# Scores and state products on four quarters of the array, and the second tile's state products next to the last chunk's scores

## The chip, the cores and the metric

The kernel runs on one core of a Trainium2 chip. The metric is the device time of one launch in microseconds (us), the median of several runs.

## The reference

One layer of a network on x of 4 sequences x 2048 tokens x 512 features: an attention with decaying state (32 heads of 16 features, chunks of 64 tokens), then a feed-forward part of 2048 hidden units. Cut to what matters, for one chunk and all heads:

```
att = rc @ kc * w_mat                  # scores, 64 x 64 per head, masked by decay
yc  = att @ vc + rc @ state * wb       # from the chunk, and from the state before it
new_state = ws * state + kc * wk @ vc  # the state product of the chunk ("kv")
```

r, k, v and a gate g come from four projections of mixed, normalized tokens; y is normalized per head, gated, projected by Wo and added to x; the feed-forward part is `x + gelu(norm(x) @ W0.T + b0) @ W1.T + b1`. The state is zero at the start of each sequence.

## The kernel before

The work goes in 32 steps of 256 tokens (`BT`), each of two tiles t of 128 tokens, each of two chunks of 64 tokens, so four chunks c = 0 to 3 a step. The attention of step n stands in one loop body with the feed-forward part of step n - 2 and with the tail (gate, Wo, residual) of step n - 1: `in_step` (L739) says what a step has, and 35 steps are issued in all. The order of each engine's work is written out by hand: `pe_step` (L1134) for TensorE, `dve_steady` (L1401) and `dve_step` for VectorE, `act_steady` (L1742) for ScalarE, `pool_step` for GpSimd, `sp_steady` (L2024) for the DMA queue of SyncE. Engines meet at counting semaphores (`s_...`). Products in higher precision than 16 bits are made as three passes over high and low halves (`PASSES`).

Features are spread over the 128 partitions so that k and r of a group g (8 heads; four groups) have the even heads of the group on partitions 0 to 63 and the odd heads on 64 to 127, for every group alike. `sp_stack` (L1981) copies them by DMA into `kx` and `rx`, with zeros between heads.

The small matmuls, which the change touches, and how they use the array of 128 rows (contracted partitions) by 128 columns (output partitions):

- Scores, `pe_scores` (L912, matmul in L926), once a chunk: 32 matmuls of 64 rows, 64 columns and 64 moving elements. The even head of a pair goes from rows 0 to 63 into columns 0 to 63, the odd one from rows 64 to 127 into columns 64 to 127. The first 16 fill one PSUM bank of `sc` (x = 0), the next 16 the other (x = 1), each half with its own wait on the weighing of the chunk before (`s_am`) and its own signal (`s_sc`).
- Attention times values, `pe_att_v` (L931, L947 and L950), once a tile: 64 matmuls of 128 rows and 64 columns, with 64 and 32 moving elements in turn. They write banks 0 and 2 of the PSUM tensor `YT`. Bank 2 (`T32`) also takes the state product of a tile's first chunk, so the group waits for that chunk's masking on VectorE (`s_km`, count 2t + 1).
- From the state, `pe_from_state` (L955, L966), right behind: 24 matmuls of 128 rows, 64 columns and 128 moving elements into bank 1, where the state product of the second chunk had been (wait on `s_km`, 2t + 2).
- State products, `pe_kv` (L971, L990), once a tile: 24 matmuls of 64 rows (a chunk's tokens), 128 columns and 128 moving elements. They give, for each group of 8 heads, all products of 128 by 128 features, also those between different heads.

In a steady step TensorE's order around them is: up 3, scores 0, kv of tile 0, G, up 4, scores 1, up 5, G, up 6, attention and from-state of tile 0, scores 2, up 7, Wo, kv of tile 1, down 0, scores 3, down 1, Wo, down 2, attention and from-state of tile 1, down 3 ("up" is L1045, 16 matmuls of 128x256; "down" is L1109, 8 of 128x512; G and the other projections are L864 and L896; Wo is L1017).

VectorE takes the scores (`dve_weigh`, L1310) and splits them (`dve_weights_lo`, L1316), and for the state of each chunk (`dve_state`, L1319) multiplies the 128x512 product by `headmask`, which leaves the products within a head (L1327, L1329 for the last chunk), and adds it to the faded state in four instructions of 128x128 (L1341). ScalarE (L1696) and GpSimd (L1942) copy the state `S` of 128x512 into 16-bit halves `Shl`. `dve_take_y` (L1352) weighs the part from the state (L1357) and adds the two from the chunk (L1365, L1367).

Before the steps, `prepare` loads and transposes the weights; `load` (L455) brings the matrices of k and r in four DMAs each, one a group, in the feature order named above.

Of the kernel before, what the change touches and what calls it, by code (L numbers as in the profile page):

```python
# [8 lines left out]
ALU = mybir.AluOpType  # L9
# [72 lines left out]

def by_head(ap):
    return ap.rearrange("p (h d) -> p h d", h=H)

def program(nc, ctx, a, consts, x, out, wd, nb):
# [34 lines left out]
    headmask = sb("headmask", [P, P])  # L122
# [27 lines left out]
    YT = ps("YT", [P, 3, C])  # L150
    Y = YT[:, 0:2, :]
# [272 lines left out]
    def prepare():  # L424
# [8 lines left out]
        tabs = sb("tabs", [P, 3 * Q + 2 + 8], F32, own)  # L433
        dist, after, same = (tabs[:, Q * k:Q * k + Q] for k in range(3))
        ages = tabs[:, 3 * Q:3 * Q + 2]
        mine = tabs[:, 3 * Q + 2:3 * Q + 10]
# [15 lines left out]
        def full(u):  # L452
            return 16 * G if u in (K_, R_) else 16
# [62 lines left out]
        def dve_exponents(eng):  # L516
            eng.wait_ge(s_tab, 48)
            eng.tensor_scalar(wb[:, :], en[:, :], ages[:, 0:1], None, ALU.mult).then_inc(s_n, 1)
            eng.tensor_scalar(wk[:, :], en[:, :], ages[:, 1:2], None, ALU.mult).then_inc(s_n, 1)
            for p in range(2):  # L520
                half = slice(Q * p, Q * p + Q)
                eng.tensor_copy(up[half, :], un[half, p:H:2]).then_inc(s_n, 1)
            eng.tensor_tensor(en_mine[:, :, :], en[:, :].rearrange("p (g h) -> p g h", g=G),
                              mine.unsqueeze(1).to_broadcast([P, G, 8]), ALU.mult).then_inc(s_n, 1)
# [180 lines left out]
    kv = sb("kv", [P, C])  # L705
    S = sb("S", [P, C])
    Shl = sb("Shl", [P, 2, 2, C], F16)
# [51 lines left out]
    def pe_piece_mean(eng, k):  # L759

        eng.wait_ge(s_ones, 1)
        if k == 0:
            eng.wait_ge(s_psq, PIECES)
            eng.wait_ge(s_wlo, 9)
            sums = f_sum[:, 0:PIECES]
        else:
            eng.wait_ge(s_yi, NT)
            eng.wait_ge(s_pm, 1)
            sums = f_most[:, :]
# [117 lines left out]
    def pe_V(eng, n, t):  # L887
        if due(NT * n):
            eng.wait_ge(s_yi if t else s_y, NT * n)
# [22 lines left out]
    def pe_scores(eng, n, c):  # L912
# [5 lines left out]
        for x in range(2):  # L918
            if c:
                eng.wait_ge(s_am, 8 * n + 2 * (c - 1) + x + 1)  # L920
            for gg in range(2):
                g = 2 * x + gg
                for q in range(4):
                    for p in range(2):
                        head = slice(Q * p, Q * p + Q)
# [3 lines left out]
            mm.then_inc(s_sc, 1)  # L929

    def pe_att_v(eng, n, t):  # L931
# [23 lines left out]
    def pe_from_state(eng, n, t):  # L955

        eng.wait_ge(s_km, NCH * n + 2 * t + 2)
# [4 lines left out]
        for g in range(G):  # L962
            for i, (a, b) in enumerate(PASSES):
                for cc in range(2):
                    at = P * t + Q * cc
                    mm = eng.matmul(Y[Q * cc:Q * cc + Q, 1, rows(g)], rT[:, a, g, at:at + Q],  # L966
                                    Shl[:, cc, b, rows(g)], start=(i == 0), stop=(i == 2))
                    if g == G - 1 and i == 2:
                        mm.then_inc(s_in, 1)

    def pe_kv(eng, n, t, ahead):  # L971
# [162 lines left out]
    def pe_step(eng, n):  # L1134
# [184 lines left out]
    def dve_state(eng, n, c):  # L1319
# [4 lines left out]
        src = (Y[:, 1, :] if c % 2 else T32).rearrange("p (g c) -> p g c", g=G)  # L1324
        mask = headmask[:, :].unsqueeze(1).to_broadcast([P, G, P])
# [26 lines left out]
    def dve_take_y(eng, n, t):  # L1352
        eng.wait_ge(s_in, NCH * n + 2 * t + 2)
        eng.wait_ge(s_av, NCH * n + 2 * t + 2)
        if due(NT * n + t):
            eng.wait_ge(s_gs, NT * n + t)
        eng.tensor_tensor(by_head(yi[:, :]), by_head(Y[:, 1, :]), wb[:, :].unsqueeze(2).to_broadcast([P, H, N]),  # L1357
                          ALU.mult).then_inc(s_yi, 1)
# [3 lines left out]
        halves = YT[:, 0:3:2, :].rearrange("p k (q b d) -> p k q b d", q=8, b=2)  # L1362
# [821 lines left out]
def constants():  # L2184
# [4 lines left out]
    spread = 32 * (r % 4) + N * (r // Q) + r % Q // 4  # L2189
# [3 lines left out]
        "headmask": same_head[spread],  # L2193
        "tabs": np.concatenate([
            np.maximum(i - j - 1, 0), (i > j) * ATT_S, (i == j) * ATT_S, -(r % Q)[:, None], -(Q - 1 - r % Q)[:, None],
            2 * (r % 4)[:, None] + r[:, None] // Q == np.arange(8)[None, :]], 1).astype(np.float32),
# [23 lines left out]
```

## Time and profile before

| | |
|---|---|
| median of 3 runs | 2111.5 us (2108.79 to 2116.0) |
| span of the profiled execution (first to last instruction) | 2113.0 us; its time apart from the span is not given |
| TensorE: matmuls / weight loads busy | 98% / 70% |
| VectorE / ScalarE / GpSimd busy | 85% / 62% / 18% |
| DMA queue of SyncE, share of 16 engines | 76.5% |
| TensorE's granted clock, mean | 0.995 |

Busy time of TensorE is a sum over matmuls whose ends are modelled and which overlap; the distance from the start of one group to the start of the next says what room a group takes. A clock of 1 is 2.4 GHz, one of 0.5 is 1.2 GHz. "Idle before" is time in which an engine had nothing running, with what ended it.

### The profile page before, as it was taken

The page shows a single profiled execution, that of the slowest core. Times are in us where ns is not written, and L with a number is a line of the kernel's source. Part 1 is how long each engine was busy: PE and PEld are TensorE (multiplying, and loading weights), DVE is VectorE, ACT ScalarE, POOL GpSimd, SP SyncE. Part 2 cuts the span into 40 slices and gives each one's busy share as a digit, 9 for nine tenths or more (in the row PEclk, how much of TensorE's full clock was granted, in tenths as well). Part 3 has the DMA queues.
Part 4 walks back from the last instruction along what each step waited for, and adds up shares of the span by engine and source line. Part 5 has one row for each costly group of instructions (what it writes and reads, how often), then busy time and mean ns, then how long its engine had stood idle before and what let it go on. Part 6 is the DMA issues. An engine that isn't in the chain of part 4 may idle for free.

```text
span 2113.0 us, 58603 instructions
## 1 busy us (share of the span) xinstructions
PE 2063.0 (98%) x24134; PEld 1479.5 (70%) x24134; DVE 1804.0 (85%) x3623; ACT 1320.0 (62%) x2081; POOL 388.0 (18%) x329
## 2 busy tenths in 40 slices
PE   5989999999999999999999999999999999999998
PEld 5777667777766777766777776676776677777665
DVE  7889889888888989888988988898988889898761
ACT  7876556667655667665656765666766566676442
POOL 1111111221211121111122111112221211211120
PEclk8999999999999999999999999999999999999999
DMA  6977777788776788777778877777887777887676
GB/s 211 229 193 234 185 217 220 224 245 235 210 215 212 225 239 241 224 209 220 218 223 245 236 216 214 223 223 224 245 232 198 227 214 222 243 236 213 206 248 231
DMA packets 428892, 471.61 MB, mean 223 GB/s; under 512 B 259409, under 2 KB 309329, under 8 KB 428625
## 3 DMA queue, kind: packets, MB, share of 16 engines
q1 hardware_dynamic: 426992, 467.64, 76.5%
q8 instruction: 192, 3.15, 0.6%
q14 instruction: 76, 0.61, 0.1%
q10 hardware_dynamic: 1632, 0.21, 0.1%
HBM read 316.24 MB, written 25.17 MB: 162 GB/s over the span
## 4 chain that ended last, share of the span: by engine, by line
PE 89%; DVE 3%; ACT 2%; DMA 2%; SPq 2%; issue 1%; ACTq 0%; DVEq 0%
PE F L1109 20%; PE F L1045 19%; PE B L864 11%; PE B L1017 8%; PE sc L864 7%; PE YT L896 7%; PE YT L864 3%; PE sc L926 3%; PE YT L947 2%; PE YT L990 2%; PE YT L966 2%; PE YT L1045 1%; PE F L821 1%; DMA y<-ygT 1%; PE YT L950 1%
## 5 line engine op out<-in xcount | busy, mean ns | idle before, releaser
L1109 PE MATMUL F<-ring,hT 128*128 128x512 f16 x1984 | 468.0, 380 | 0.0
L1045 PE MATMUL F<-xT,ring 128*128 128x256 f16 x3840 | 450.1, 273 | 6.6 <-issue 3.9
L1045 PEld LDWEIGHTS F<-xT,ring 128*128 128x128 f16 x3840 | 369.9, 98 | 66.3 <-issue 9.5
L1109 PEld LDWEIGHTS F<-ring,hT 128*128 128x128 f16 x1984 | 186.7, 98 | 195.3
L1739 ACT ACTIVATE hT<-F,b,f_rho 128x256 f16<-128x256 f32 x480 | 243.8, 560 | 81.8 <-PE F L1045 81.8
L1942 POOL TENSOR_TENSOR Shl<-S,Shl 128x512 f16<-128x512 f32 x128 | 156.4, 1222 | 739.8 <-ACT Shl L1696 739.8
L864 PE MATMUL B<-mix,WT 128*128 128x256 f16 x2304 | 267.6, 273 | 1.2 <-DVE gT L1348 1.2
L1696 ACT ACTIVATE Shl<-S 128x512 f16<-128x512 f32 x128 | 80.6, 630 | 283.0 <-PE YT L966 161.0
L864 PEld LDWEIGHTS B<-mix,WT 128*128 128x128 f16 x2304 | 222.6, 98 | 36.4 <-DVE gT L1348 1.5
L267 DVE SCALAR_TENSOR_TENSOR mixf<-dx,maa,xnT 128x256 f32<-128x256 f32 x512 | 238.8, 527 | 0.1
L1316 DVE TENSOR_TENSOR att<-att 128x512 f16<-128x512 f32 x256 | 180.2, 745 | 16.0 <-ACT att L1690 15.9
L327 DVE TENSOR_TENSOR mix<-mixf,mix 128x1024 f16<-128x1024 f32 x128 | 184.1, 1438 | 2.7 <-ACT mix L323 1.6
L864 PE MATMUL sc<-mix,WT 128*128 128x256 f16 x1536 | 179.6, 274 | 2.9 <-PEq L551 2.9
L896 PE MATMUL YT<-WT,mix 128*128 128x512 f16 x768 | 177.8, 382 | 1.1 <-DVE mix L327 0.7
L1017 PE MATMUL B<-WT,yg 128*128 128x512 f16 x768 | 176.2, 379 | 0.0
L1310 DVE TENSOR_TENSOR att<-sc,wmask 128x512 f32<-128x512 f32 x256 | 164.3, 684 | 12.8 <-PE sc L926 12.8
L864 PEld LDWEIGHTS sc<-mix,WT 128*128 128x128 f16 x1536 | 150.8, 98 | 34.0 <-issue 3.1
L1947 POOL TENSOR_TENSOR x<-e,x 128x512 f32<-128x512 f16 x62 | 70.8, 1162 | 556.4 <-DVE e L1383 556.4
L1690 ACT ACTIVATE att<-att 128x512 f16<-128x512 f32 x256 | 147.2, 623 | 19.0 <-DVE att L1310 17.7
L1341 DVE SCALAR_TENSOR_TENSOR S<-S,ws,kv 128x128 f32<-128x128 f32 x384 | 142.8, 433 | 3.9 <-POOL Shl L1942 0.5
L323 ACT ACTIVATE mix<-mixf 128x1024 f16<-128x1024 f32 x128 | 134.4, 1050 | 4.8 <-DVE mixf L267 3.9
L896 PEld LDWEIGHTS YT<-WT,mix 128*128 128x128 f16 x768 | 75.2, 98 | 86.3 <-issue 2.6
(196 smaller groups left out, 3066.9 us busy)
## 6 DMA issues: line engine op xcount, KB each, us to landing
ring<-w_dram SPq DMA_DIRECT2D x512, 512.0 KB, 4.6
kx<-kT SPq DMA_DIRECT2D x96, 256.0 KB, 3.9
rx<-rT SPq DMA_DIRECT2D x96, 256.0 KB, 4.5
xa<-in_L_attn_x SPq DMA_DIRECT2D x32, 512.0 KB, 7.2
vbd<-vN SPq DMA_DIRECT2D x256, 64.0 KB, 2.9
x<-in_L_attn_x SPq DMA_DIRECT2D x32, 512.0 KB, 6.2
out<-x SPq DMA_DIRECT2D x31, 512.0 KB, 4.0
w_dram<-ring SPq DMA_DIRECT2D x20, 256.0 KB, 3.8
```

What stands on the lines that cost most here:

```text
L267: last = eng.scalar_tensor_tensor(out=mixf[:, m % 2, g, :], in0=dx[:, g, :], scalar=maa[:, m, g:g + 1], in1=xnT[:, g, 1:BT + 1], op0=ALU.m ...
L327: eng.tensor_tensor(mix[:, m % 2, 1, :, :], mixf[:, m % 2, :, :], mix[:, m % 2, 0, :, :], ALU.subtract).then_inc(s_ml, 1)
L864: mm = eng.matmul(out[:, gg * BT:(gg + 1) * BT], WT[:, w, a, kk, rows(g)], mix[:, m % 2, b, kk, :], start=(i == 0 and kk == 0), stop=(i == ...
L896: mm = eng.matmul(Y[:, t, :], mix[:, 0, a, kk, rows(t)], WT[:, V_, b, kk, :], start=(i == 0 and kk == 0), stop=(i == 2 and kk == G - 1))
L1017: mm = eng.matmul(B[:, :], yg[:, a, kk, rows(t)], WT[:, O_, b, kk, :], start=(i == 0 and kk == 0), stop=(i == 2 and kk == G - 1))
L1045: mm = eng.matmul(up_place(f, j)[:, i * BT:(i + 1) * BT], ring[:, use % RING, i, a * C + kk * P:a * C + (kk + 1) * P], xT[:, :, kk, :], st ...
L1109: mm = eng.matmul(F[:, t, :], hT[:, k, rows(t)], ring[:, use % RING, i, a * C:(a + 1) * C], start=(k == 0 and a == 0), stop=(k == NH - 1 a ...
L1310: eng.tensor_tensor(att32[:, x, :], sc[:, x, :], wmask[:, 8 * x:8 * x + 8, :].rearrange("p q i -> p (q i)"), ALU.mult).then_inc(s_am, 1)
L1316: eng.tensor_tensor(att[:, c % 2, 1, C * x:C * x + C], att32[:, x, :], att[:, c % 2, 0, C * x:C * x + C], ALU.subtract).then_inc(s_al, 1)
L1690: eng.activation(att[:, c % 2, 0, C * x:C * x + C], att32[:, x, :], ACT.Copy).then_inc(s_ah, 1)
L1739: eng.activation(hT[:, k, :], up_place(f, j)[:, i * BT:(i + 1) * BT], ACT.Gelu, bias=b0[:, k:k + 1], scale=f_rho[:, j:j + 1]).then_inc(s_h, 1)
L1942: eng.tensor_tensor(Shl[:, b, 1, :], S[:, :], Shl[:, b, 0, :], ALU.subtract).then_inc(s_Sl, 1)
```

## The change

Scores, from-state and kv matmuls all become 64 rows by 64 columns with 64 moving elements, and follow one another over the four quarters of the array. For groups 2 and 3 the even heads now lie on partitions 64 to 127 and the odd ones on 0 to 63 (`rows_of`). From-state and kv go from 24 matmuls to 48; the state and its product keep only the rows and columns of one parity, so `kv`, `S` and `Shl` are half as wide (256 in place of 512). The PSUM tensor `YT` is divided anew, the attention group waits for both chunks' masking, and `dve_take_y` weighs in two instructions. The kv of tile 1 moves from behind Wo to behind down 0, directly ahead of scores 3. The first two weight matrices are loaded in six DMAs each. Tables (`headmask`, `tabs`) follow the new feature order; their part of the diff is left out.

```diff
+def rows_of(g, p):
+    half = p if g < 2 else 1 - p
+    return slice(Q * half, Q * half + Q)
...
     YT = ps("YT", [P, 3, C])
+    BY_PARITY = YT[:, :, :].rearrange("p b c -> p (b c)").rearrange("p (k s c) -> p k s c", k=2, s=3)
+    FROM_STATE = BY_PARITY[:, :, 0, :]
+    FROM_CHUNK = BY_PARITY[:, :, 1:3, :].rearrange("p k s c -> p k (s c)")
...
         def load(eng, u):
...
                 for b in range(G):
-                    eng.dma_start(raw[:, u, b, :], source[b]).then_inc(landed[u], 16)
+                    if b < 2:
+                        eng.dma_start(raw[:, u, b, :], source[b]).then_inc(landed[u], 16)
+                    else:
+                        for p in range(2):
+                            at = rows_of(b, p)
+                            eng.dma_start(raw[at, u, b, :], source[b][N * p:N * p + N]).then_inc(landed[u], 16)
...
-    kv = sb("kv", [P, C])
-    S = sb("S", [P, C])
-    Shl = sb("Shl", [P, 2, 2, C], F16)
+    kv = sb("kv", [P, C // 2])
+    S = sb("S", [P, C // 2])
+    Shl = sb("Shl", [P, 2, 2, C // 2], F16)
...
     def pe_V(eng, n, t):
         if due(NT * n):
-            eng.wait_ge(s_yi if t else s_y, NT * n)
+            eng.wait_ge(s_y, NT * n)
...
     def pe_scores(eng, n, c):
...
-        for x in range(2):
-            if c:
-                eng.wait_ge(s_am, 8 * n + 2 * (c - 1) + x + 1)
-            for gg in range(2):
-                g = 2 * x + gg
-                for q in range(4):
+        if c:
+            eng.wait_ge(s_am, 8 * n + 2 * c)
+        for gg in range(2):
+            for q in range(4):
+                for x in range(2):
                     for p in range(2):
-                        head = slice(Q * p, Q * p + Q)
+                        g = 2 * x + gg
+                        head = rows_of(g, p)
                         mm = eng.matmul(sc[Q * p:Q * p + Q, x, gg * BT + Q * q:gg * BT + Q * q + Q],
                                         kx[head, q, g, Q * c:Q * c + Q], rx[head, q, g, Q * c:Q * c + Q],
                                         start=True, stop=True)
-            mm.then_inc(s_sc, 1)
+                    if gg == 1 and q == 3:
+                        mm.then_inc(s_sc, 1)
...
     def pe_att_v(eng, n, t):
...
-        eng.wait_ge(s_km, NCH * n + 2 * t + 1)
+        eng.wait_ge(s_km, NCH * n + 2 * t + 2)
...
-                    pair = YT[Q * cc:Q * cc + Q, 2 * (q // 8), at:at + 4 * N]
+                    pair = FROM_CHUNK[Q * cc:Q * cc + Q, q // 8, at:at + 4 * N]
...
     def pe_from_state(eng, n, t):
-        eng.wait_ge(s_km, NCH * n + 2 * t + 2)
...
             for i, (a, b) in enumerate(PASSES):
-                for cc in range(2):
-                    at = P * t + Q * cc
-                    mm = eng.matmul(Y[Q * cc:Q * cc + Q, 1, rows(g)], rT[:, a, g, at:at + Q],
-                                    Shl[:, cc, b, rows(g)], start=(i == 0), stop=(i == 2))
+                for p in range(2):
+                    for cc in range(2):
+                        at = P * t + Q * cc
+                        mm = eng.matmul(FROM_STATE[Q * cc:Q * cc + Q, rows_of(g, p).start // Q, Q * g:Q * g + Q],
+                                        rT[rows_of(g, p), a, g, at:at + Q], Shl[rows_of(g, p), cc, b, Q * g:Q * g + Q],
+                                        start=(i == 0), stop=(i == 2))
...
+    def kv_place(c):
+        return Y[:, 1, C // 2:C] if c % 2 else T32[:, 0:C // 2]
...
     def pe_kv(eng, n, t, ahead):
...
-                    dst = Y[:, 1, rows(g)] if cc else T32[:, rows(g)]
-                    mm = eng.matmul(dst, kN[part, a, g, t, :], vw[part, t, b, rows(g)],
-                                    start=(i == 0), stop=(i == 2))
+                    for p in range(2):
+                        row = rows_of(g, p)
+                        mm = eng.matmul(kv_place(cc)[row, Q * g:Q * g + Q], kN[part, a, g, t, row],
+                                        vw[part, t, b, rows(g)].rearrange("p (q a d) -> p a q d", a=2, d=N)[:, p],
+                                        start=(i == 0), stop=(i == 2))
...
     def pe_step(eng, n):
...
-        if att_n:
-            pe_kv(eng, n, 1, n < STEADY)
         if ff:
             pe_down(eng, n - 2, 0)
         if att_n:
+            pe_kv(eng, n, 1, n < STEADY)
             pe_scores(eng, n, 3)
...
     def dve_state(eng, n, c):
...
-        mask = headmask[:, :].unsqueeze(1).to_broadcast([P, G, P])
+        mask = headmask[:, :].unsqueeze(1).to_broadcast([P, G, 4 * N])
...
-            last = eng.scalar_tensor_tensor(out=S[:, rows(g)], in0=S[:, rows(g)], scalar=fading[:, g:g + 1],
-                                            in1=kv[:, rows(g)], op0=ALU.mult, op1=ALU.add)
+            at = slice(Q * g, Q * g + Q)
+            last = eng.scalar_tensor_tensor(out=S[:, at], in0=S[:, at], scalar=fading[:, g:g + 1],
+                                            in1=kv[:, at], op0=ALU.mult, op1=ALU.add)
...
     def dve_take_y(eng, n, t):
...
-        eng.tensor_tensor(by_head(yi[:, :]), by_head(Y[:, 1, :]), wb[:, :].unsqueeze(2).to_broadcast([P, H, N]),
-                          ALU.mult).then_inc(s_yi, 1)
+        for x in range(2):
+            at = slice(C // 2 * x, C // 2 * x + C // 2)
+            last = eng.tensor_tensor(yi[:, at].rearrange("p (k a d) -> p a k d", a=2, d=N),
...
+        last.then_inc(s_yi, 1)
```

## Rows read from the trace of the kernel before

**Rows 1.** The page: span; busy time, share, instructions of three engines; granted clock

```profile
span 2113.0 us, 58603 instructions
...
PE 2063.0 (98%) x24134; PEld 1479.5 (70%) x24134; DVE 1804.0 (85%) x3623; ACT 1320.0 (62%) x2081; POOL 388.0 (18%) x329
...
PEclk8999999999999999999999999999999999999999
```

**Rows 2.** Timeline, TensorE, a middle step: start us, length us, line, operation, count

```profile
1004.84 0.69 PE L926 MATMUL sc<-rx,kx 64*64 64x64 f16 x32
1005.46 0.84 PE L990 MATMUL YT<-vw,kN 64*128 64x128 f16 x24
...
1008.87 1.91 PE L1045 MATMUL F<-xT,ring 128*128 128x256 f16 x16
1010.71 0.69 PE L926 MATMUL sc<-rx,kx 64*64 64x64 f16 x32
1011.33 1.92 PE L1045 MATMUL F<-xT,ring 128*128 128x256 f16 x16
...
1017.60 0.19 PE L950 MATMUL YT<-vbd,att 128*64 128x32 f16 x2
1017.63 0.20 PE L947 MATMUL YT<-vbd,att 128*64 128x64 f16 x2
...
1018.59 0.84 PE L966 MATMUL YT<-Shl,rT 128*64 128x128 f16 x24
1019.36 0.69 PE L926 MATMUL sc<-rx,kx 64*64 64x64 f16 x32
...
1024.42 0.85 PE L990 MATMUL YT<-vw,kN 64*128 64x128 f16 x24
1025.20 1.90 PE L1109 MATMUL F<-ring,hT 128*128 128x512 f16 x8
...
1033.80 0.22 PE L947 MATMUL YT<-vbd,att 128*64 128x64 f16 x2
...
1066.99 0.69 PE L926 MATMUL sc<-rx,kx 64*64 64x64 f16 x32
...
1082.13 2.17 PE L1045 MATMUL F<-xT,ring 128*128 128x256 f16 x16
```

**Rows 3.** Timeline, VectorE, the same step

```profile
1005.32 1.29 DVE L1310 TENSOR_TENSOR att<-sc,wmask 128x512 f32<-128x512 f32 x2 [0.26 <-PE sc L926]
...
1026.71 0.68 DVE L1327 TENSOR_TENSOR kv<-YT,headmask 128x512 f32<-128x512 f32 x1
1027.43 1.14 DVE L1341 SCALAR_TENSOR_TENSOR S<-S,ws,kv 128x128 f32<-128x128 f32 x4
1028.48 1.28 DVE L1310 TENSOR_TENSOR att<-sc,wmask 128x512 f32<-128x512 f32 x2
...
1031.54 0.74 DVE L1329 SCALAR_TENSOR_TENSOR kv<-YT,flag,headmask 128x512 f32<-128x512 f32 x1
```

**Rows 4.** Groups by line and shape, VectorE: busy us, mean ns, idle before

```profile
L1327 DVE TENSOR_TENSOR kv<-YT,headmask 128x512 f32<-128x512 f32 x96 | 65.6, 684 | 0.9 <-PE YT L990 0.9
...
L54 DVE SCALAR_TENSOR_TENSOR rs_t<-rs_t,rs_a 128x68 f32<-128x68 f32 x87 | 19.9, 229 | 3.0
...
L1399 DVE TENSOR_TENSOR x<-e,x 128x256 f32<-128x256 f16 x2 | 0.9, 426 | 0.1
```

**Rows 5.** Timeline, SyncE's queue, the step after: the weights' transfers

```profile
1074.13 1.87 SPq L1978 DMA_DIRECT2D ring<-w_dram  x3
```

**Rows 6.** The page: DMA issues, KB each, median us from issue to landing

```profile
ring<-w_dram SPq DMA_DIRECT2D x512, 512.0 KB, 4.6
```

**Rows 7.** Timeline of the start, TensorE and SyncE's queue

```profile
1.77 3.20 SPq L460 DMA_DIRECT2D raw<-in_L_attn_Wk  x4
...
11.03 1.94 PE L591 MATMUL F<-ident,raw 128*128 128x128 f32 x8 [11.03 <-DMA raw<-in_L_attn_Wk]
...
70.34 1.13 PE L821 MATMUL F<-xT,ring 128*128 128x128 f32 x8 [2.02 <-ACT vw L802]
```

More of the change, by code:

```diff
@@ L121, in program @@
     wmask = sb("wmask", [P, NT * 8, Q])
-    headmask = sb("headmask", [P, P])
+    headmask = sb("headmask", [P, 4 * N])
     wb = sb("wb", [P, H])
@@ L432, in prepare @@
         means = sb("means", [P, P], F32, own)
-        tabs = sb("tabs", [P, 3 * Q + 2 + 8], F32, own)
+        tabs = sb("tabs", [P, 3 * Q + 2 + 16], F32, own)
         dist, after, same = (tabs[:, Q * k:Q * k + Q] for k in range(3))
         ages = tabs[:, 3 * Q:3 * Q + 2]
-        mine = tabs[:, 3 * Q + 2:3 * Q + 10]
+        mine = tabs[:, 3 * Q + 2:3 * Q + 18].rearrange("p (x h) -> p x h", x=2)
         ep = sb("ep", [P, NT * 8], F32, own)
@@ L452, in full @@
         def full(u):
-            return 16 * G if u in (K_, R_) else 16
+            return 16 * (G + 2) if u in (K_, R_) else 16
         def load(eng, u):
@@ L522, in dve_exponents @@
                 eng.tensor_copy(up[half, :], un[half, p:H:2]).then_inc(s_n, 1)
-            eng.tensor_tensor(en_mine[:, :, :], en[:, :].rearrange("p (g h) -> p g h", g=G),
-                              mine.unsqueeze(1).to_broadcast([P, G, 8]), ALU.mult).then_inc(s_n, 1)
+            eng.tensor_tensor(en_mine[:, :, :].rearrange("p (x g) h -> p x g h", x=2),
+                              en[:, :].rearrange("p (x g h) -> p x g h", x=2, g=2),
+                              mine.unsqueeze(2).to_broadcast([P, 2, 2, 8]), ALU.mult).then_inc(s_n, 1)
             eng.wait_ge(s_n, 5)
@@ L766, in pe_piece_mean @@
         else:
-            eng.wait_ge(s_yi, NT)
+            eng.wait_ge(s_y, NT)
             eng.wait_ge(s_pm, 1)
@@ L963, in pe_from_state @@
             for i, (a, b) in enumerate(PASSES):
-                for cc in range(2):
-                    at = P * t + Q * cc
-                    mm = eng.matmul(Y[Q * cc:Q * cc + Q, 1, rows(g)], rT[:, a, g, at:at + Q],
-                                    Shl[:, cc, b, rows(g)], start=(i == 0), stop=(i == 2))
-                    if g == G - 1 and i == 2:
-                        mm.then_inc(s_in, 1)
+                for p in range(2):
[4 more added lines that the diff above has]
+                                        start=(i == 0), stop=(i == 2))
+                        if g == G - 1 and i == 2 and p == 1:
+                            mm.then_inc(s_in, 1)
+    def kv_place(c):
+        return Y[:, 1, C // 2:C] if c % 2 else T32[:, 0:C // 2]
     def pe_kv(eng, n, t, ahead):
@@ L1356, in dve_take_y @@
             eng.wait_ge(s_gs, NT * n + t)
-        eng.tensor_tensor(by_head(yi[:, :]), by_head(Y[:, 1, :]), wb[:, :].unsqueeze(2).to_broadcast([P, H, N]),
-                          ALU.mult).then_inc(s_yi, 1)
+        for x in range(2):
+            at = slice(C // 2 * x, C // 2 * x + C // 2)
+            last = eng.tensor_tensor(yi[:, at].rearrange("p (k a d) -> p a k d", a=2, d=N),
+                                     FROM_STATE[:, :, P * x:P * x + P].rearrange("p a (k d) -> p a k d", d=N)[:, ::1 - 2 * x],
+                                     wb[:, H // 2 * x:H // 2 * x + H // 2].rearrange("p (k a) -> p a k", a=2).unsqueeze(3).to_broadcast(
+                                         [P, 2, H // 4, N]), ALU.mult)
+        last.then_inc(s_yi, 1)
         eng.wait_ge(s_yi, NT * n + t + 1)
@@ L1361, in dve_take_y @@
             eng.wait_ge(s_yT, NT * n)
-        halves = YT[:, 0:3:2, :].rearrange("p k (q b d) -> p k q b d", q=8, b=2)
+        halves = FROM_CHUNK.rearrange("p k (q b d) -> p k q b d", q=8, b=2)
         dst = y[:, t, :].rearrange("p (k q d) -> p k q d", k=2, q=8)
@@ L2188, in constants @@
     same_head = (r[:, None] // N == r[None, :] // N).astype(np.float32)
-    spread = 32 * (r % 4) + N * (r // Q) + r % Q // 4
+    own = 2 * (r % 4)[:, None] + np.stack([r // Q, 1 - r // Q], 1)
     return {
@@ L2192, in constants @@
         "centring": (np.eye(P) - same_head / N).astype(np.float32),
-        "headmask": same_head[spread],
+        "headmask": ((r % 4)[:, None] == np.arange(4 * N)[None, :] // N).astype(np.float32),
         "tabs": np.concatenate([
             np.maximum(i - j - 1, 0), (i > j) * ATT_S, (i == j) * ATT_S, -(r % Q)[:, None], -(Q - 1 - r % Q)[:, None],
-            2 * (r % 4)[:, None] + r[:, None] // Q == np.arange(8)[None, :]], 1).astype(np.float32),
+            (own[:, :, None] == np.arange(8)[None, None, :]).reshape(P, 16)], 1).astype(np.float32),
     }
```

2 lines of the change are left out of this document (1 added, 1 removed).

## The prediction

> **What bounds the kernel now.** I read the page first: TensorE is busy for 98% of the span at a granted clock of nearly 1, VectorE for 85% [rows 1]. A matmul's busy time can hide pace, so I went on to TensorE's timeline in a step of the middle [rows 2]. From one step's first scores to the next step's is 1066.99 - 1004.84 = 62.15 us; 18 of the 31 such distances are 62.15 to within 0.02, and inside the step every group starts where the one before leaves off. So steady steps (29 of the 32 that do attention) are TensorE work laid end to end, and what the change is worth is the room that its groups take there, start to start, not their busy time.
>
> **Pace of the small matmuls.** 32 scores take 0.69 us; less the last one's own 0.19 that is 0.50 us from first to last start, 0.033 us for each of 15 pairs (two tiles of 64x64, on the diagonal). The state products through L966 and L990 go in pairs of 128 columns: (0.84 - 0.22) / 11 = 0.056 us a pair, 0.67 us for 12. The attention times values groups alternate pairs of 64 columns (L947) and of 32 (L950), and both follow at the same pace: 31 pairs from 1017.60 to 1018.59, 0.032 us each [rows 2]. So 0.031 to 0.033 us is what one pair of 64-wide tiles costs even when it streams half as much; it does not come from columns streamed alone. What the change asks is whether four tiles fit into that time as two do.
>
> **Cost of changing the tiling.** 16 full matmuls before the scores start at 1008.87, pace (1.91 - 0.27) / 15 = 0.109 us, 1.75 us in all, but the scores start 1.84 us later: 0.09 us extra. Scores hold 0.62 us of room (1010.71 to 1011.33) for 16 x 0.033 = 0.53: again 0.09. From scores to the state products of another shape, 1004.84 to 1005.46, it is the same [rows 2]. I take 0.09 us for each change of shape.
>
> **The change, part by part, per steady step.**
> 1. *Scores, four groups.* The same 32 matmuls, now ordered over four quarters: 8 rounds in place of 16 pairs. At the pair's pace for a round: 8 x 0.032 = 0.25 us less, 1.0 us for four.
> 2. *Products from the state, two groups.* 24 matmuls of 128 columns become 48 of 64 on quarters, 12 rounds. At 0.032: 0.38 in place of 0.67 us, 0.29 less, 0.58 for two.
> 3. *State products (kv), two groups.* The same counts, shape and saving: 0.58 us. Their moving operand now comes in runs of 16 elements; that of L947 does too and keeps 0.032, so nothing for it.
> 4. *Changes of shape.* Before there are 14 in a step. The first kv group now has the shape of the scores ahead of it (one fewer), the second is moved next to the last scores (two fewer), the products from the state no longer share the shape of the attention group: for the first tile this trades one change for another, for the second it adds one. 12 in all, 2 x 0.09 = 0.18 us less.
> 5. *Waits.* Faster bursts shorten the time in which TensorE's sequencer can work off the kv group's waits behind the scores; no row prices this. Bounds: nothing, or the room of one change of shape, 0.09, which I take.
>
> Sum: 1.0 + 0.58 + 0.58 + 0.18 - 0.09 = 2.25 us a step. The other bound is two at a time: rounds give nothing, scores stay, and 48 matmuls at 0.016 are 0.75 in place of 0.67, so 4 x 0.08 = 0.32 us more, less 0.18: 0.14 us more a step. One at a time (0.03 each, 5 us more a step) I exclude: rows show pairs side by side that differ in columns (L947), in rows (L990) and in both (L926) [rows 2], and in the new order such pairs still follow each other. I take the first bound since each kind of neighbour that four quarters need is already seen to overlap; only all of them at once is not shown.
>
> **Is it hidden or given back?** VectorE runs nearly without a pause from 1005.32 to 1032.3, and the second attention group needs its work [rows 2, 3]. It gets shorter too: the masking goes from 512 to 256 elements (0.68 to 0.43 us by the 256-wide row), the state updates from 128 to 64 wide (near 0.23 each by the 68-wide row; now four take 1.14 us in a chain, so 0.2 to 0.3 less), about 0.5 us a chunk [rows 4]; `dve_take_y` gets one instruction more, 0.15. ScalarE's and GpSimd's half-size copies of the state lie beside other work: nothing. The new wait: the attention group now needs both chunks masked (`s_km` + 2). In the second tile that is the instruction at 1031.54, ending 1032.28, against a start at 1033.80: 1.5 us to spare. TensorE arrives 2.25 - 0.29 = 2.0 earlier, VectorE 3 x 0.5 + 0.25 - 0.15 = 1.6, so 1.1 remain. The move: kv starts at 1024.42 - 1.3 (saved so far) + 1.83 (the down group, 1025.20 on) = 1024.95 and is done near 1025.5; VectorE asks for it at 1026.71 - 1.0 + 0.15 = 1025.9 [rows 2, 3]. Nothing waits, and the last scores behind it are no later. No DMA moves with it; SP's queue passes nothing new. Weights: the last up group's transfer is issued at 1074.13, lands 4.6 us after 0.6 of issuing, at 1079.3, and is wanted at 1082.13; TensorE comes 1.3 earlier, 1.5 us remain [rows 5, 6]. The waits in `pe_V` and on both `s_am` cost nothing: the first is reached by the group ahead, the second is met 4 us before 1010.71.
>
> **Outside the steady steps.** The first three steps have idle stretches that wait for ScalarE, as the 2 us before 70.34 [rows 7]; between 0 and 6.8 us of their savings arrive, I take 3. At the start, two more transfers of the first weight matrix stand in SP's queue and TensorE waits for that matrix until 11.03; four took 3.2 us, so 1.6 more if half-size ones cost as much; the second matrix adds two before the third is issued, partly covered. 0 to 4 us, I take 2 [rows 7].
>
> Total: 29 x 2.25 = 65, + 3, - 2 = 66 us less. The sum is made against the profiled execution, of which the span of 2113.0 is all that is given [rows 1]; the median of the runs, 2111.5, lies 1.5 below it, within their scatter of 2108.8 to 2116.0, so the difference is carried over as it is. 2111.5 - 66 = 2045.5, said as **2046 us**.
>
> **Rivals.** *Two at a time* (0.11). Something that tiles share lets only two matmuls start in 0.032 us: 0.14 x 32 + 2 = 6.5 us slower, 2118, just beyond what can be told from no change (0.3%, here 6.3 us). Its place is the scores and state groups, and it decides from a round of about 0.06 us on. For it: no row has four. Against it: the pairs of every kind. 
>
> *A new wait* (0.08). The attention group in the second tile ends up behind VectorE (if VectorE saved nothing, 0.5 us a step, 15 us), or weights land late by up to 1 us, 29 us: 2061 to 2075.
>
> *Four at a time* (0.72), the forecast: its own range is 2035 to 2057, from the bounds of the start (2), the early steps (3), item 5 (3) and a round of 0.031 or 0.033 (80 rounds a step, 3).
>
> The range 2030 to 2084 holds the forecast, the new wait and most of the case in between, some 0.85. Faster: 0.72 + 0.09 + 0.08 = 0.89; the last rival splits around its edge, 0.05 same and 0.06 slower.
>
> **What would show it.** Right: 32 scores in about 0.42 us from first start to last end, 48 matmuls of L966's and L990's successors in about 0.54 to 0.57; distances of steps near 59.9; the second kv group directly ahead of the last scores with no gap; DVE's masking rows near 0.43. Wrong: scores still at 0.69 and state groups near 0.95 (two at a time); small groups short but the step still over 61, with idle time of TensorE ahead of the attention group put down to the masking, or to a ring transfer (a new wait).

## The result, and the profile after

| | before | after |
|---|---|---|
| median (runs) | 2112.03 us (4: 2108.79 to 2116.0) | 2099.02 us (4: 2098.03 to 2100.3) |
| profiled execution: span | 2113.0 us | 2096.2 us (its device time is 2098.03) |
| granted clock, mean | 0.995 | 0.988 |

The ratio is 0.9934 with a 95% interval of 0.9919 to 0.9949: 13 us or 0.7% faster, where the prediction said 66 us and a range that ended at 2084. From the page of after, beside [rows 1] and [rows 6]: the span, the busy times, queue q8 that was not looked at before, one group of matmuls with its idle time, and the weights' transfer.

```profile
span 2096.2 us, 64752 instructions
...
PE 2009.1 (96%) x27206; PEld 1432.4 (68%) x27206; DVE 1739.2 (83%) x3687; ACT 1292.4 (62%) x2081; POOL 317.8 (15%) x329
...
q8 instruction: 216, 3.54, 0.7%
...
L1068 PE MATMUL F<-xT,ring 128*128 128x256 f16 x3840 | 459.0, 276 | 16.6 <-issue 12.1
...
ring<-w_dram SPq DMA_DIRECT2D x512, 512.0 KB, 4.6
```

TensorE's busy time fell by 54 us and its share from 98% to 96%: it now stands idle for some 87 us where it was 50. The timeline of TensorE shows where. First a step with nothing in its way (start us, length us, line, operation, count):

```profile
1000.32 0.45 PE L941 MATMUL sc<-rx,kx 64*64 64x64 f16 x32
1000.63 0.57 PE L1012 MATMUL YT<-vw,kN 64*64 64x64 f16 x48
...
1005.61 0.45 PE L941 MATMUL sc<-rx,kx 64*64 64x64 f16 x32
1005.99 1.92 PE L1068 MATMUL F<-xT,ring 128*128 128x256 f16 x16
...
1013.32 0.58 PE L982 MATMUL YT<-Shl,rT 64*64 64x64 f16 x48
1013.73 0.46 PE L941 MATMUL sc<-rx,kx 64*64 64x64 f16 x32
1014.13 1.92 PE L1068 MATMUL F<-xT,ring 128*128 128x256 f16 x16
```

From these scores to those of the next step, at 1060.26 below, is 59.94 us, against 62.15 before [rows 2]. This is the time forecast for every steady step. In the next step something else happens:

```profile
1060.26 0.45 PE L941 MATMUL sc<-rx,kx 64*64 64x64 f16 x32
...
1073.28 0.57 PE L982 MATMUL YT<-Shl,rT 64*64 64x64 f16 x48
1073.69 0.23 PE L941 MATMUL sc<-rx,kx 64*64 64x64 f16 x5
1077.07 0.41 PE L941 MATMUL sc<-rx,kx 64*64 64x64 f16 x27 [3.16 <-issue]
1077.42 1.92 PE L1068 MATMUL F<-xT,ring 128*128 128x256 f16 x16
...
1083.58 0.57 PE L1012 MATMUL YT<-vw,kN 64*64 64x64 f16 x48
1083.98 0.21 PE L941 MATMUL sc<-rx,kx 64*64 64x64 f16 x4
```

In the middle of a group of 32 matmuls, which has no wait inside it, TensorE stops for 3.16 us, and the view gives "issue" as the reason: it waited for nothing that the profile shows. The next scores 0 start at 1123.54, 63.28 us later. TensorE's waits in all (what waited, for what: us in total, times, longest us), of after:

```profile
PE sc L941 <- issue: 22.3, 8, 3.5
PE F L1068 <- issue: 12.1, 5, 3.4
...
PE B L1040 <- issue: 5.1, 3, 2.6
PE F L1068 <- ACT hT L1767: 4.1, 9, 0.8
```

and of the kernel before:

```profile
PE F L1045 <- issue: 3.9, 4, 1.3
...
PE sc L926 <- issue: 1.6, 2, 1.0
```

So it had such stops too, six in these rows and short.

**What stands at those places.** Numbering the trace's records of TensorE (loads, matmuls and the sequencer's waits, 55,257 in all), every "issue" stop of over 1 us in the steady steps of the changed kernel lies at the same place of a block of 256, at record 193 or 194 of it. In the kernel before, five of the six lie there too; the sixth, 1.09 us at 182.68, is ahead of the steady steps and does not, nor does a seventh, of 1.05 us at 2043.44, near the end. The page has the other side: q8, kind "instruction", moved 216 transfers of 16 KB, and 55,257 / 256 is 215.8. Before, 49,176 / 256 is 192.1, and its q8 has 192:

```profile
q8 instruction: 192, 3.15, 0.6%
```

In *pad_hit* below, with 58,337 records (227.9 blocks), q8 has 228. So q8 brings in TensorE's own program, 256 instructions at a time. The DMA queues in two stretches of the stop above (packets, MB, share of 16 engines):

```profile
q1 hardware_dynamic: 458, 1.21, 101.8%
...
ring<-w_dram SPq DMA_DIRECT2D x1, 512.0 KB, 7.7
```

```profile
q1 hardware_dynamic: 272, 0.58, 101.6%
q8 instruction: 1, 0.02, 4.0%
```

The first is 1071.5 to 1074.5: data fill all sixteen engines, a weight transfer takes 7.7 us in place of the usual 4.6, and no instructions come. The second is 1074.5 to 1076: the block comes (by its record from 1074.55, in 0.96 us), and TensorE goes on at 1077.07.

**The bookkeeping.** From step 3 to step 31 the mean distance is 61.87 us (before 62.49, its smallest 62.15). That is 28 x 0.62 = 17 us gained; on top of 59.94 the kernel loses 28 x 1.93 = 54 us, where the one before lost 28 x 0.34 = 9.5 on top of its 62.15. The gaps at the block boundary, each taken from the last start before it to the first behind it, are 40.6 us in 16; the one in the last step, 2.8 us, lies outside these 28 distances, so they make some 38 of the 54. Of the rest, up to 14 can be what follows them: the trace has 27 us at half clock in these steps. By windows (us; busy of PE, PEld, DVE, ACT, POOL, each with its count; granted clock; DMA share; GB/s), the stretch with the end of the stop of 2.63 us that began at 516.3:

```profile
517.00:523.00 6.00, 4.07 (x12) 1.51 (x12) 4.79 (x7) 2.04 (x4) 0.00 (x0) 0.72 0.59 235
```

TensorE, at full clock until it stopped, gets 1.2 GHz for part of it; so behind 8 of the 13 stops of over 1.5 us from step 2 on. The first scores come 1.7 us later, step 3 starts 1.95 us later, and the part behind the last step's first scores is 1.5 us shorter.

### The profile page after: what moved, and what is told of

The parts are those of the page before. It is cut to its first block, busy times and chain, and to the rows that moved or that the text cites. A ratio compares the mean times of both kernels' runs of the same rounds, so it can differ in the third digit from the quotient of the medians.

```text
span 2096.2 us, 64752 instructions
## 1 busy us (share of the span) xinstructions
PE 2009.1 (96%) x27206; PEld 1432.4 (68%) x27206; DVE 1739.2 (83%) x3687; ACT 1292.4 (62%) x2081; POOL 317.8 (15%) x329
## 4 chain that ended last, share of the span: by engine, by line
PE 77%; SPq 5%; DVE 4%; issue 4%; ACT 4%; DMA 4%; POOL 0%; ACTq 0%; DVEq 0%
PE F L1132 19%; PE F L1068 15%; PE B L879 9%; PE B L1040 8%; PE sc L879 7%; PE YT L911 5%; PE YT L879 3%; DMA y<-ygT 3%; PE YT L963 2%; SPq L2026 2%; PE sc L941 2%; PE YT L982 2%; PE F L836 1%; PE YT L1012 1%; SPq L2013 1%
## 5 line engine op out<-in xcount | busy, mean ns | idle before, releaser
L1068 PE MATMUL F<-xT,ring 128*128 128x256 f16 x3840 | 459.0, 276 | 16.6 <-issue 12.1
L1724 ACT ACTIVATE Shl<-S 128x256 f16<-128x256 f32 x128 | 53.4, 417 | 257.4 <-PE YT L982 140.4
L1970 POOL TENSOR_TENSOR Shl<-S,Shl 128x256 f16<-128x256 f32 x128 | 89.4, 698 | 756.9 <-ACT Shl L1724 756.9
L1338 DVE TENSOR_TENSOR att<-att 128x512 f16<-128x512 f32 x256 | 166.8, 693 | 39.2 <-ACT att L1718 39.0
L1040 PE MATMUL B<-WT,yg 128*128 128x512 f16 x768 | 180.7, 385 | 5.1 <-issue 5.1
L1040 PEld LDWEIGHTS B<-WT,yg 128*128 128x128 f16 x768 | 76.3, 99 | 92.5 <-issue 11.3
L1653 ACT ACTIVATE kT<-sc 128x512 f16<-128x512 f32 x64 | 38.1, 596 | 154.7 <-PE sc L879 154.7
```

Of the source, the lines that this page charges most:

```text
L1040: mm = eng.matmul(B[:, :], yg[:, a, kk, rows(t)], WT[:, O_, b, kk, :], start=(i == 0 and kk == 0), stop=(i == 2 and kk == G - 1))
L1068: mm = eng.matmul(up_place(f, j)[:, i * BT:(i + 1) * BT], ring[:, use % RING, i, a * C + kk * P:a * C + (kk + 1) * P], xT[:, :, kk, :], st ...
L1338: eng.tensor_tensor(att[:, c % 2, 1, C * x:C * x + C], att32[:, x, :], att[:, c % 2, 0, C * x:C * x + C], ALU.subtract).then_inc(s_al, 1)
```

## The experiments

The theory: TensorE uses up 256 instructions in a stretch of small matmuls faster than the next block arrives, where DMA is full. Attention, from-state and scores 2 were 240 instructions in about 2.4 us and are 288 in about 1.9. Only steps in which the block's end falls 226 to 338 instructions behind the first product of attention times values of tile 0 should stop for long. The trace of the changed kernel bears it out: from step 2 on 15 boundaries lie 226 to 339 behind it and all stop (0.65 to 3.5 us idle), while those at 218 and at 346 and all others do not. In the kernel before, the steady stops lie at 223 to 270. A step has 1688 instructions (6 x 256 + 152), so the place moves from step to step. Rivals: the new waits, the work's new order, or that four quarters are not truly at work.

### Moving the place of the boundary, and nothing else

*pad_clear* and *pad_hit* repeat 52 scores matmuls in scores 1 of every steady step (the results are overwritten by the same values), so that a step has 1792 = 7 x 256 instructions. They differ in step 3 alone, by which the boundary stays clear of the small matmuls or always falls among them.

```diff
+        extra = 0 if c != 1 or n < 3 else 16 if n == 3 else 52     # pad_hit: 84 in place of 16
+        for k in range(extra):
...
+            eng.matmul(sc[...], kx[head, q, g, ...], rx[head, q, g, ...], start=True, stop=True)
```

> The changed kernel with 52 of the scores' matmuls of chunk 1 made twice in each steady step (16 in the first), so that a step holds 1792 = 7 x 256 instructions of TensorE and every attention group of the first tile starts at the same place between two multiples of 256 instructions. Here that place is one where the profile of the changed kernel shows no stall (a boundary 130 instructions behind the group's first matmul). Theory 'instruction supply': the 3 us stalls are TensorE waiting for its next 256 instructions, so none longer than 0.7 us is left in the steady steps, a step takes 59.94 + 13 rounds x 0.032 = 60.4 us, and the time is 2055 to 2068. Rival 'data supply' (weights or inputs land late behind the faster stretch): alignment of instructions changes nothing, about 14 stalls stay, 2099 + 12 = 2111.

> The same as pad_clear but for 68 more matmuls made twice in the first steady step, which puts the boundary 250 instructions behind the group's first matmul, the place of the long stalls. 'Instruction supply': every steady step stalls, 29 x about 3.0 us, and some lose up to 1.7 us more at half clock: 2145 to 2200. 'Data supply': the same time as pad_clear, 2111, both with about 14 stalls.

Measured: pad_clear **2056.08 us** (2055.44 to 2057.35; ratio 0.9726, 0.9711 to 0.974), pad_hit **2212.74 us** (2204.57 to 2217.81; ratio 1.0462, 1.0434 to 1.0491). The same work, and 157 us apart by 68 matmuls in one step. Their waits of TensorE (pad_clear, then pad_hit):

```profile
PE F L1075 <- issue: 2.5, 2, 1.4
...
PE sc L948 <- issue: 0.8, 1, 0.8
```

```profile
PE sc L948 <- issue: 91.5, 29, 3.7
```

pad_clear's two waits of L1075 lie in steps 1 and 2, ahead of the repeats; 0.8 us is its only stop at a boundary in the steady steps. pad_hit has 29 steps and 29 stops, near 3.2 us each. It came out above its expectation, and the clock goes with it: the mean granted clock is 0.966, against 0.995. Its timeline of one step, and the same stretch by windows:

```profile
1129.08 0.29 PE L948 MATMUL sc<-rx,kx 64*64 64x64 f16 x13
1132.78 0.48 PE L948 MATMUL sc<-rx,kx 64*64 64x64 f16 x19 [3.41 <-issue]
1133.19 3.19 PE L1075 MATMUL F<-xT,ring 128*128 128x256 f16 x16
1136.21 2.75 PE L1047 MATMUL B<-WT,yg 128*128 128x512 f16 x12
```

```profile
1119.00:1129.00 10.00, 10.00 (x257) 8.56 (x257) 8.91 (x17) 10.00 (x20) 2.95 (x3) 1.00 0.92 311
1133.00:1136.00 3.00, 3.00 (x33) 2.18 (x26) 2.42 (x3) 0.00 (x0) 0.00 (x0) 0.53 0.27 105
1137.00:1140.00 3.00, 3.00 (x16) 1.36 (x14) 2.02 (x4) 1.99 (x4) 0.00 (x0) 1.00 0.47 175
```

Behind the stop the clock falls to 1.2 GHz, and sixteen large matmuls take 3.02 us from start to start in place of 1.75. A stop of 3.4 us so costs at least 4.7. On average a steady step of pad_hit is 5.7 us longer than one of pad_clear (66.16 against 60.48), and its trace has 133 us at half clock in them, where pad_clear's has none. pad_clear's median step is 60.47 us, and its repeats take 0.44 (timeline below): 60.03 for the work itself, where the prediction said 62.15 - 2.25 = 59.90.

```profile
1048.38 0.61 PE L940 MATMUL sc<-rx,kx 64*64 64x64 f16 x52
1048.82 0.61 PE L948 MATMUL sc<-rx,kx 64*64 64x64 f16 x32
```

### The same boundary in the kernel before

*before_clear* and *before_hit* repeat 19 scores matmuls a step (1536 = 6 x 256), again differing in step 3 only.

```diff
+            extra = 0 if c != 1 or x or n < 3 else 69 if n == 3 else 19     # before_hit: 10 in place of 69
```

> The kernel before with 19 repeated scores matmuls (two at a time, 0.017 us each: 0.32 us a step) in each steady step's scores of chunk 1, and 69 in step 3, so that a step has 1536 = 6 x 256 TensorE instructions and the 256-instruction boundary lies 131 instructions behind the first product of att_v of chunk 0. Theory (the boundary stalls TensorE where 256 instructions in a row are short): no step has the boundary in the dangerous place. The repeats cost about 29 x 0.32 + 0.8 = 10 us, and the few short stalls that the kernel before has (some 6 to 9 us in all) go: about 2114, 2108 to 2120. Rival (alignment is worth as much in any kernel, some 40 us): 2080 to 2090.

> The same with 10 repeats in step 3, so that the boundary lies 249 behind the first product of att_v of chunk 0 in each steady step. Theory: the kernel before runs the 256 instructions ahead of that boundary in about 2.4 us where the changed one needs about 1.9, so its stall there is the 0.8 to 1.5 us of its own trace in place of 3.4: 2112 + 9 + 29 x (0.8 to 1.5) = 2145 to 2165, with the clock at full speed. Rival (the two kernels suffer alike from the same place of the boundary, and the change as such has no part in it): 29 x 3.4 = 98 and half-clock stretches more, 2210 to 2230.

Measured: before_clear 2113.82 us (2111.99 to 2116.35; ratio 1.0003, 0.9994 to 1.0013) as expected; before_hit 2124.08 us (2120.8 to 2131.19; ratio 1.0061, 1.0043 to 1.0079), far below its expectation of 2145 to 2165: the 256 instructions took 3.3 us and not 2.4, and their block came early (table below). The same place costs the old kernel 10 us and the changed one 157. At that place the block ends inside the scores of chunk 2 in the changed kernel, and in the first matmuls of up 7, right behind them, in the kernel before. The waits of before_hit:

```profile
PE F L1051 <- issue: 7.3, 14, 1.3
```

### Less on the DMA queue, and the small matmuls further apart

*quiet* holds the transfer of `xa` and one of the ring back until scores 2 are done, and with them what is queued behind; *spread* issues scores 2 behind up 7; *quiet_spread* has both. No repeats in these three, so the boundary wanders as in the changed kernel.

```diff
-        for i in range(7, 10):
+        for i in range(7, 9):                 # quiet
...
+        eng.wait_ge(s_sc, 8 * n + 6)          # then the ring transfer and xa
+        sp_weights(eng, use + 9)
...
-            pe_scores(eng, n, 2)              # spread
         if ff:
             pe_up(eng, n, 7)
+            pe_scores(eng, n, 2)
```

> The changed kernel with the transfers of the next input tile and of one block of weights (and what is queued behind them) held back until the scores of chunk 2 are done, so that fewer data transfers stand ahead of the instructions' own. 'Instruction supply': the fetch lands sooner, the stalls of 3 us shrink to below 2 us, time 2065 to 2085, unless a weights block now comes late. 'A fixed cost of a fetch' (its length does not depend on what the DMA engines carry): no change, 2095 to 2102. 'Data supply': later transfers make it slower than 2099.

> The changed kernel with the scores of chunk 2 moved behind the last up group, so that the longest run of small matmuls is 224 instructions and not 288, under one block of 256. 'Instruction supply': each window of 256 instructions now holds at least 32 instructions of full matmuls, 1.7 us more for the fetch; a stall of 3.2 us becomes 1.5, about 15 x 1.7 = 25 us less, one change of shape more per step (29 x 0.09 = 3 us): 2070 to 2085. 'Data supply': VectorE's and the weights' waits are as they were, 2100 to 2104.

> The changed kernel with both measures and no repeated matmuls: transfers held back and the scores of chunk 2 behind the last up group. 'Instruction supply': the run of small matmuls leaves 1.7 us more for a fetch that now takes about 1 us less, so most of the 12 stalls that quiet still had (22 us) end: 2072 - 18 + 3 = 2050 to 2062. If the two measures overlap (a fetch waits either way), no better than quiet, 2070.

Measured: quiet 2072.64 us (2070.73 to 2076.61; 0.9809, 0.979 to 0.9829) and spread 2083.08 us (2079.05 to 2085.88; 0.9851, 0.9832 to 0.987), both as 'instruction supply' expected, and quiet_spread 2063.44 us (2057.07 to 2066.5; 0.976, 0.973 to 0.9789), just above its expectation. The gaps at the boundary, 16 of 40.6 us in the changed kernel, are 12 of 19.9, 17 of 25.2, and 8 of 8.1 us. Each measure works alone, and together they give most of their sum: by the ratios 1.7%, where the two alone give 1.25% and 0.8%.

The same two measures at the bad place, on top of pad_hit:

> The changed kernel with repeats that put the 256-instruction boundary 250 behind the first product of attention times values of tile 0 in each steady step (as in pad_hit), and the two data transfers nearest to that place (a ring transfer and xa) issued only once scores 2 are done. Theory (the block of instructions is fetched by DMA and stands behind data transfers): the stall falls from 3.3 us to the 1.7 that the version with held transfers alone showed a gap, 29 x 1.6 = 46 us less than 2213, and with fewer half-clock stretches 10 to 20 less again: 2140 to 2175. Rival (the stall is a fixed latency of the fetch, whatever the DMA engines carry): 2205 to 2220.

> The changed kernel with the boundary at the same place as in pad_hit, 250 behind the first product of attention times values of tile 0, but scores 2 moved behind up 7, so that the last 26 of those instructions belong to 16 large matmuls of 0.109 us each and the 256 before the boundary take about 2.8 us rather than 1.9. Theory (what counts is the time that the 256 instructions before the boundary take): stalls of 0 to 1 us a step, 2056 + 0.5 x 29 = 2060 to 2090. Rival (the place of the boundary in the block as such stalls): 2205 to 2220.

Measured: hit_quiet 2151.47 us (2139.61 to 2155.23; 1.0176, 1.0146 to 1.0207), inside its range; hit_spread 2140.79 us (2133.98 to 2145.53; 1.0143, 1.0126 to 1.016), far above its own and far below the rival's. Waits of hit_quiet, then of hit_spread (two of whose 30 lie ahead of the steady steps):

```profile
PE sc L948 <- issue: 53.1, 28, 2.9
```

```profile
PE F L1075 <- issue: 47.8, 30, 2.1
```

I had taken 2.8 us of work ahead of the boundary for nearly enough; it was 3.4, and is not. The records say why. Medians over the stalled boundaries (stops over 0.8 us; for before_hit all) of the steps between 400 and 1950 us, each time counted from the boundary before (a stop is counted from the last start before it to the first behind it, some 0.2 us more than the idle time in the views):

| kernel | the 256 took | fetch begins | and takes | TensorE goes on after its end | stop |
|---|---|---|---|---|---|
| before (4) | 3.5 | 2.3 | 0.9 | 1.4 | 1.1 |
| changed (12) | 2.4 | 3.2 | 1.0 | 1.45 | 3.1 |
| pad_hit (24) | 2.04 | 3.1 | 1.0 | 1.4 | 3.6 |
| hit_quiet (25) | 2.04 | 1.7 | 1.0 | 1.4 | 2.0 |
| hit_spread (25) | 3.37 | 3.1 | 1.0 | 1.4 | 2.1 |
| before_hit (24) | 3.29 | 1.2 | 1.0 | about 1.4 | 0.2 |

Each stop is what the fetch needs less what the 256 instructions give: for pad_hit 3.1 + 1.0 + 1.4 - 2.04 = 3.5, for hit_quiet 2.1, for hit_spread 2.1, for before_hit 0.3. So by these medians a block needs 5.5 us from the boundary before it in pad_hit, of which 3.1 are a wait to begin, and 4.1 in hit_quiet. There is one fetch for each boundary: paired in order, nine in ten of the changed kernel's begin between 1.8 us ahead of their boundary and 3.6 us behind it, and the latest 5.6 us behind (400 to 1950 us). In hit_quiet the fetch begins as the data run dry: over 25 boundaries its start follows the moment at which at most two of the engines still move data with a correlation of 0.84. With less data issued the fetch begins sooner, and it begins as they run dry: it is behind the data that the fetch waits. **Open** stays why it begins after 1.2 us in before_hit, where data fill the engines as well; of the distance between before_hit and hit_spread, whose 256 take nearly as long, it makes all of the 1.9 us. One thing goes with it in the records: the transfers of `x` and `xa` are issued 2.8 and 2.4 us ahead of that boundary in before_hit, but 1.8 and 1.4 us ahead of it in pad_hit and hit_spread (medians). Data queued ahead of the fetch thus had 1 us longer to move, which would be about half of the 1.9; no run changes this alone.

### Are four quarters truly at work, and what is the move worth?

All three on top of pad_clear. *scores_pairs* orders the 32 scores by half (x outside), so that in each half only two quarters alternate; *state_pairs* does the like for from-state and kv; *move_back* puts kv of tile 1 back ahead of down 0.

```diff
-        for gg in range(2):
-            for q in range(4):
-                for x in range(2):
+        for x in range(2):                    # scores_pairs
+            for gg in range(2):
+                for q in range(4):
...
+            pe_kv(eng, n, 1, n < STEADY)      # move_back
         if ff:
             pe_down(eng, n - 2, 0)
         if att_n:
-            pe_kv(eng, n, 1, n < STEADY)
             pe_scores(eng, n, 3)
```

> pad_clear, but the scores ordered as before the change: all of one half of sc, then all of the other, so that only two tiles at a time differ. Same instructions, same place of the boundaries. If a round of four costs what a pair does (0.032 us), 8 rounds more for each of four groups: 1.0 us a step, 0.69 us a group, and about 2056 + 32 = 2088. If the gain came from something else (fewer waits on the weighing), 2056 to 2060.

> pad_clear, but in the products from the state and the state products the loop over the halves p stands outside, so that neighbours are pairs (one row half with both column halves; for the state products both row halves into one column half) instead of four quarters. 12 rounds more at 0.032 us for each of four groups: 1.5 us a step, 0.95 us a group, 2056 + 48 = 2104. If it is the narrower state alone that pays (VectorE, ScalarE, GpSimd), 2056.

> pad_clear, but the second tile's state products back behind Wo, ahead of down 0. Two changes of shape more at 0.09 us: 0.18 us a step, 29 steps, 2056 + 5 = 2061. If a change of shape costs nothing between groups on quarters, 2056.

Measured: 2069.82 us (2067.58 to 2072.34; 0.9798, 0.9773 to 0.9822), 2075.37 us (2075.22 to 2079.55; 0.9826, 0.98 to 0.9852) and 2071.82 us (2069.11 to 2077.77; 0.9807, 0.9781 to 0.9833). The first two go the expected way and lose 14 and 19 us against pad_clear, where 32 and 48 were expected. Rows of scores_pairs, then of state_pairs:

```profile
1061.55 0.57 PE L948 MATMUL sc<-rx,kx 64*64 64x64 f16 x32
```

```profile
1051.16 0.45 PE L948 MATMUL sc<-rx,kx 64*64 64x64 f16 x32
1051.52 0.75 PE L1019 MATMUL YT<-vw,kN 64*64 64x64 f16 x48
```

Scores take 0.57 where four quarters take 0.45 and pairs took 0.69 [rows 2]; state products 0.75 in place of 0.57. The four quarters are used at once, and the order of issue matters: but where the order passes from one half to the other, the records show the second half's first tiles starting while the first half's still run (in the scores above, the two matmuls that open the second half start 0.137 and 0.140 us after the group, though the first half's pairs go on to 0.190), which gives back part of the loss. *move_back* lost 16 us where 5 were expected: its median step is 60.99 us, where pad_clear's is 60.47. Its smallest, step 3 as in pad_clear, is 60.26 against 60.07: 0.19 us more, the two changes of shape that were expected at 0.18, some 5 us in all. Part of the rest is again the supply of instructions, at another boundary, 386 behind the attention products, which now falls into kv:

```profile
PE YT L1019 <- issue: 3.8, 8, 0.7
```

Where the remaining 7 us or so come from was not taken apart.

## Why the prediction was wrong

The mechanism of the saving held, and so did its size in an undisturbed step; what failed is the sentence that the sum stands on.

- **Four at a time: right.** Scores are 0.45 us long where 0.42 was forecast, and 48 state products 0.57 against 0.54 to 0.57; rounds of four start 0.032 to 0.033 us apart. From-state of tile 0 holds 0.41 us of room (1013.32 to 1013.73) where it held 0.77. An undisturbed step is 2.21 us shorter, against 2.25 for items 1 to 5.
- **The rivals.** *Two at a time* is out, with both rules of the Trainium skill that spoke for it: the "TensorE: Matmul & The Clock Gate" rule that a weight load overlaps only with another row group, and "TensorEngine Tiling (Array Packing)", Gotcha 1, would both leave scores at 0.69. *In between* is out by the same rows.
- **A new wait: one came, but neither of those named.** The rival named the masking and the weights. Neither shows: in the list of waits none is for a mask, and the ring's median landing is still 4.6 us. Masking went to 0.42 us (L1349, 417 ns; 0.43 forecast), the four updates of the state from 1.14 to 0.87 us:

```profile
1022.01 0.87 DVE L1364 SCALAR_TENSOR_TENSOR S<-S,ws,kv 128x64 f32<-128x64 f32 x4
```

- **The step that failed: "steady steps are TensorE work laid end to end, and what the change is worth is the room that its groups take there".** TensorE also needs its instructions, and the prediction had no term for them. The change adds 96 matmuls and as many loads a step (1498 to 1688 records, with two waits fewer), all of them in the groups that it makes quicker, and 48 of these instructions in the run that stops. Item 5 looked at what the sequencer must work off, but only at waits. The rows were there: 192 transfers of kind "instruction" on the page, and six waits for "issue" of up to 1.3 us in the kernel before, two of them in the scores; the prediction said nothing of these 5.5 us. The sum, for the two profiled executions (2113.0 to 2096.2, 16.8 less where 66 were forecast): the 28 distances of steps gave 17 in place of 28 x 2.25 = 63. Of the 46 missing, 54 - 9.5 = 44.5 are what the changed kernel loses to stops and what follows them beyond what the kernel before lost, and 1 is the undisturbed step. The start and the early steps miss 3 more, the end 0.8. The medians lie 13 apart, a little less than this pair.
- **Outside the steady steps.** The start cost 1.7 us of the 2 that I took. Four transfers took 3.20 us [rows 7]; the six take 1.32 + 3.23:

```profile
1.77 1.32 SPq L470 DMA_DIRECT2D raw<-in_L_attn_Wk  x2
3.13 3.23 SPq L474 DMA_DIRECT2D raw<-in_L_attn_Wk  x4
```

  The early steps gave nothing (3 forecast): step 3 starts 1.95 us later than before, 1.7 of it from the start. One stop at a boundary, 1.83 us at 210.45 in step 2, is among what they lost. The end gave 1.5.
- **Without the stops** the forecast is nearly borne out: pad_clear is 2056.08, its repeats are 28 x 0.44 and 0.1 in step 3, 12 us, which leaves 2044 (worked out, not run) against 2046. Part of that nearness is luck: the stops are taken out of the changed kernel alone, while the kernel before keeps its own short ones. Like with like: before_clear is 2113.82 and its repeats 28 x 0.32 and 1.1 in step 3, 10 us, which leaves 2104; so with the stops out of both, the change is worth 60 us where 66 were forecast.

The Trainium skill, "Runtime: NRT & Kernel Launch", Instruction fetch mechanics, says that an engine's instructions are refilled in blocks of 256 and that this is hidden, since instructions are dispatched more slowly than they are filled in. The first agrees with q8's counts; the second does not hold here: 29 stops of 3.2 us.

The best version run is pad_clear, 2.7% faster than before and 2.0% faster than the change alone. It is fragile: an edit that adds or takes away TensorE instructions ahead of the steady steps moves its boundary, and pad_hit, 68 matmuls on, is 4.6% slower than before. The version with held transfers and scores 2 apart (2063.44) goes through all places and stops for 8.1 us in all, at most 1.9 us idle at a time; it was not run held at the worst.

## What to carry to other kernels

Smaller and more numerous matmuls are paid for in instructions: where a stretch runs 256 of an engine's instructions in less than the 5.5 us that a block needed here while the DMA engines were full, look for waits for "issue" inside groups that have no wait, and number the records to see whether they are a block apart. Before such a change is judged, move the boundary with a few harmless instructions; here that alone made 2.7% faster out of 4.6% slower. What helped here is less data in flight at that time, the short bursts set apart, and a step of a whole number of blocks with the boundary clear of the bursts.

## What was not expected of the hardware

- TensorE's program comes by DMA in 16 KB blocks behind the data in flight: a fetch began up to 3.2 us (median) behind the boundary before, took 1.0, and the engine went on 1.4 us after its end. With two data transfers held back it began after 1.7 (hit_quiet).
- A stop of 3.4 us of TensorE was followed by 1.2 GHz (0.53 granted in 1133 to 1136 us) though the engine had been busy without a pause before. It does not follow each time: the stop of 3.16 us at 1074 in the changed kernel had full clock behind it.
- Tiles of 64x64 on four quarters start 0.032 to 0.033 us apart by fours, 0.0083 us a matmul with its weight load (two quarters of each round write one PSUM bank, two another); and they overlap beyond the order of issue, so that pairs listed half by half cost 0.57 us and not 0.69.
